# The first slice of a weight matrix loaded in two column halves, with two warm-up matmuls fewer

## The chip, the cores and the metric

The kernel runs on one core of a Trainium2 chip. The metric is the device time of one execution in microseconds (us).

## The reference

x has 4096 rows of 512 (128 batches of 32). For each row the reference computes

```python
base   = x @ W.T                                  # W 512 x 512
logits = x @ Wr.T + 5.0 * one_hot(language_of_batch)   # 8 experts
gates  = softmax over the two largest logits, 0 elsewhere
h      = x @ A[e].T for each expert e             # 8 experts x 16
c      = base + 2.0 * sum_e gates[e] * h[e] @ B[e].T
out    = x + softplus(scale) * (c @ sign)         # sign 512 x 512, of +1 and -1
```

all of it in fp32.

## The kernel before, in words

The kernel folds matrices first and then runs over the rows. It computes M = softplus(scale) * (W.T @ sign) + I once, and B2 = 2 * softplus(scale) * (B @ sign) once; then each of the 32 tiles of 128 rows needs x @ [Wr, A, M] (a product of width 648, held in two PSUM banks), the gates, and a small product h_gated @ B2 that is added to the same banks. Every fp32 operand is split in a rounded high part (suffix _hi, type fp32r) and the rest (suffix _lo), and a product is the sum of three: high by high, high by low and low by high.

The order of work is written out by hand, one list for each engine, tied together with semaphores. The part around the change is the opening, in which M is summed over four slices of 128 rows of W and sign (j = 0 to 3):

- **SyncE's queue** (lines 254 to 268) issues W's slices 0 and 1, the scale, W's slices 2 and 3, sign's slice 3, then the first tile of x, A, B and further tiles of x.
- **ScalarE's queue** (line 354) issues sign's slices 0, 1 and 2, then loads its activation table (line 357), and then makes w_hi of slice 0 in two operations (lines 362 and 364), w_hi of the other slices (line 367) and sign_hi of slices 1 to 3 (line 370).
- **VectorE** (lines 468 to 473) clears buffers, waits for sign's slice 0, and makes its sign_hi in two column halves of 256 (lines 493 and 494); each half has a semaphore of its own, first_sign_made and early_sign_hi_made. Behind it in the same list come w_lo of slice 0 and 1 (low_w, line 478), the scale (lines 499 to 501), w_lo of slice 2, eight operations on one column for softplus, w_lo of slice 3, the transposes of x, A, Wr and the language numbers (lines 488 and 521 to 526), then fold(k) (line 532), which reads the four finished sums of M, and low_m (line 538), which makes wide_lo, the low part of M.
- **GpSimd** builds the diagonals and makes sign_lo of each slice (line 318), for slice 0 when early_sign_hi_made says that the second half of sign_hi is there, for the others behind ScalarE's sign_hi.
- **TensorE** first runs WARM_UPS = 19 matmuls of constants (line 657), 128 x 256 bf16, whose result isn't used. Then come slice 0's high by high in column halves (lines 692 and 696): the four matmuls of the left half wait for the first half of w_hi and for first_sign_made, the four of the right half for early_sign_hi_made. Behind them stand low_high(0) (line 677, waits for w_lo of slice 0), high_high(1) (670), high_low(0) (684, waits for sign_lo of slice 0) and so on in a fixed order, slice 3 last (lines 650 to 652), then B2 (717, 721), then the first tile of x (first_tile, line 759) and the loop over tiles (wide, line 734, and lora, line 770). lora of tile 0 waits for ht_lo (line 569).

```python
            for j in range(EARLY):                      # EARLY = 1, VectorE
                dve.wait_ge(sign_loaded[j], 16)
                nc.vector.tensor_copy(sign_hi[:, j, 0:HALF], ...).then_inc(first_sign_made, 1)
                nc.vector.tensor_copy(sign_hi[:, j, HALF:D], ...).then_inc(early_sign_hi_made, 1)
                low_w(j)
            low_w(1)
```

Of the kernel before, what the change touches and what calls it, by code (L numbers as in the profile page):

```python
# [18 lines left out]
def adaln_ffn_kernel(nc: bass.Bass, x, lang_ids, W, Wr, A, B, sign, scale, out):  # L19
# [13 lines left out]
    BATCH, TILES, D = x.shape  # L33
# [5 lines left out]
    OC = O // P  # L39
# [2 lines left out]
    Y0 = D // 2  # L42
    BANKS = ((0, 0, HEAD + Y0), (1, HEAD + Y0, WIDE))
    assert BATCH == P and ER == P and D % (NQ * Q) == 0 and HEAD + Y0 <= 512 and O == KC * P
    WARM_UPS = 19
    HALF = D // 2
    EARLY = 1
    RING = 4
# [4 lines left out]
    sign_load = sign.rearrange("(j p) n -> p j n", p=P)  # L53
# [5 lines left out]
    with ctx:  # L59
        def sb(name, shape, dt=FP32):  # L60
            return ctx.enter_context(nc.sbuf_tensor(name, shape, dt))

        def sem(name):
            return ctx.enter_context(nc.semaphore(name))
# [3 lines left out]
        sign_in = sb("sign_in", [P, OC, D])  # L68
# [13 lines left out]
        sign_hi = sb("sign_hi", [P, OC, D], FP32R)  # L82
# [48 lines left out]
        a_loaded = sem("a_loaded")  # L131
        wr_loaded = sem("wr_loaded")
        w_loaded = [sem(f"w_loaded{j}") for j in range(OC)]
        sign_loaded = [sem(f"sign_loaded{j}") for j in range(OC)]
        b_loaded = sem("b_loaded")
        scale_loaded = sem("scale_loaded")
# [20 lines left out]
        first_sign_made = sem("first_sign_made")  # L157
# [193 lines left out]
        @block.scalar  # L351
        def _(act):

            for j in range(OC - 1):
                act.dma_start(sign_in[:, j, :], sign_load[:, j, :]).then_inc(sign_loaded[j], 16)

            nc.scalar.preload_act_table_set("natural_log_exp_and_others")
# [101 lines left out]
        def _(dve):  # L459
# [15 lines left out]
            def low_w(j):  # L475

                dve.wait_ge(w_hi_made, j + 1)
                nc.vector.tensor_tensor(w_lo[:, j, :, :, :],  # L478
                                        w_in[:, j, :].rearrange("p (i k a) -> p k i a", i=NQ, k=KC),
                                        w_hi[:, j, :, :, :].bitcast(FP32), ALU.subtract).then_inc(w_lo_made, 1)  # L480
# [8 lines left out]
                                    x_in[n][:, :, :].rearrange("p g c -> p (g c)")).then_inc(xt_made, 1)  # L489

            for j in range(EARLY):
                dve.wait_ge(sign_loaded[j], 16)
                nc.vector.tensor_copy(sign_hi[:, j, 0:HALF], sign_in[:, j, 0:HALF]).then_inc(first_sign_made, 1)
                nc.vector.tensor_copy(sign_hi[:, j, HALF:D], sign_in[:, j, HALF:D]).then_inc(early_sign_hi_made, 1)
                low_w(j)
            low_w(1)
# [150 lines left out]
        def _(pe):  # L647
# [7 lines left out]

            for _ in range(WARM_UPS):
                nc.tensor.matmul(p_b2[:, 0:2 * P], nc.const_aps.tensor(1.0, [P, P], BF16),
# [205 lines left out]
```

## Time and profile before

| | us |
|---|---|
| median of 3 runs | 163.86 (163.75 to 163.94) |
| the profiled execution, its own time | 163.53 |
| its span, first to last instruction | 161.3 |
| TensorE busy in it | 157.4 (98%) |
| VectorE busy | 110.0 (68%) |
| ScalarE busy | 63.6 (39%) |
| GpSimd busy | 52.2 (32%) |

Times in the rows are microseconds from the span's start unless marked ns. PE is TensorE's matmul side, PEld its weight loads, DVE VectorE, ACT ScalarE, POOL GpSimd, SP SyncE; a q behind a name is that engine's instruction queue, and L12 is line 12 of the kernel. Durations of matmuls include the way through the array, so those of neighbours overlap, and the distance of their starts is the pace. The page's row of TensorE's granted clock stands at 9 (90% or more) in all 40 slices.

### The profile page before, as it was taken

Reading aid. Unit: us, or ns where it says so; the run is one execution under the profiler, and the core shown is the slowest. Engines: PE = TensorE matmul, PEld = TensorE weight load, DVE = VectorE, ACT = ScalarE, POOL = GpSimd, SP = SyncE. Lnnn points to the kernel's source line nnn. Section 1 sums busy time; section 2 is a strip of 40 time slices with the busy share of each in tenths; the row PEclk is TensorE's granted clock in tenths of the full one; section 3 lists DMA queues with packets and bytes.
Section 4 is the critical chain, followed back from the end, with each engine's and each line's share of the span. In section 5 each row is a group of like instructions: output and inputs, shape, how many; then the busy total and the mean of one; then the engine's idle time right before and its main releaser. Section 6 shows DMA issues by size and latency. Waiting matters only on the chain.

```text
span 161.3 us, 3653 instructions
## 1 busy us (share of the span) xinstructions
PE 157.4 (98%) x1046; PEld 151.8 (94%) x1046; DVE 110.0 (68%) x451; ACT 63.6 (39%) x178; POOL 52.2 (32%) x50
## 2 busy tenths in 40 slices
PE   8999999999999999999999999999999999999993
PEld 5887889899999999999999999999999999999992
DVE  5999999566666667666656666676666666666641
ACT  3645622244433334234344444433444343334432
POOL 2975554333330323333333333223132333333000
PEclk9999999999999999999999999999999999999999
DMA  5995332335545545344454545555555362223333
GB/s 178 376 150 131 107 107 74 89 76 150 147 142 148 142 104 180 106 135 123 126 142 136 139 142 146 143 146 145 144 146 145 86 189 81 62 62 87 130 130 130
DMA packets 45867, 21.47 MB, mean 133 GB/s; under 512 B 23680, under 2 KB 40864, under 8 KB 45856
## 3 DMA queue, kind: packets, MB, share of 16 engines
q1 hardware_dynamic: 30232, 13.58, 31.0%
q10 hardware_dynamic: 15624, 7.76, 16.6%
q8 instruction: 5, 0.08, 0.2%
q14 instruction: 6, 0.05, 0.1%
HBM read 11.03 MB, written 8.39 MB: 120 GB/s over the span
## 4 chain that ended last, share of the span: by engine, by line
PE 78%; DVE 11%; DMA 4%; issue 1%; SPq 1%; ACT 1%; ACTq 0%; DVEq 0%
PE pair L734 63%; PE pair L770 15%; DMA w_in<-in_L_cond_W 2%; DVE wide_lo L538 2%; DMA h_moved<-h_gated 2%; DVE m_full L532 2%; DVE w_lo L478 1%; DVE xt L488 1%; SPq L277 1%; DVE scale_spread L499 1%; DVE b_lo L543 1%; DVE second L616 1%; ACT w_hi L367 0%; ACT xt_hi L383 0%; DVE wide_lo L548 0%
## 5 line engine op out<-in xcount | busy, mean ns | idle before, releaser
L325 POOL TENSOR_TENSOR xt_lo<-xt,xt_hi 128x512 fp32r<-128x512 f32 x32 | 41.8, 1305 | 90.2 <-ACT xt_hi L383 90.2
L734 PE MATMUL pair<-wide_hi,xt_lo 128*128 128x392 f32 (+1 forms) x248 | 58.5, 311 | 0.0
L734 PE MATMUL pair<-wide_hi,xt_hi 128*128 128x392 f32 (+1 forms) x248 | 58.4, 311 | 0.0
L734 PE MATMUL pair<-wide_lo,xt_hi 128*128 128x392 f32 (+1 forms) x248 | 58.4, 312 | 0.0
L734 PEld LDWEIGHTS pair<-wide_hi,xt_hi 128*128 128x128 f32 x248 | 38.6, 188 | 0.4 <-issue 0.3
L734 PEld LDWEIGHTS pair<-wide_hi,xt_lo 128*128 128x128 f32 x248 | 38.6, 188 | 0.0
L734 PEld LDWEIGHTS pair<-wide_lo,xt_hi 128*128 128x128 f32 x248 | 38.5, 188 | 0.0
L447 ACT ACTIVATE y<-pair 128x256 f32<-128x256 f32 x31 | 11.9, 383 | 50.1 <-PE pair L770 50.1
L383 ACT ACTIVATE xt_hi<-xt 128x512 fp32r<-128x512 f32 x32 | 20.3, 633 | 9.7 <-DVE xt L488 7.9
L488 DVE STREAM_TRANSPOSE xt<-x_in 128x512 f32<-128x512 f32 x32 | 22.5, 703 | 0.0
L421 ACT ACTIVATE ht_hi<-ht 128x128 fp32r<-128x128 f32 x29 | 12.6, 433 | 24.1 <-DVE ht L580 24.1
L569 DVE TENSOR_TENSOR ht_lo<-ht,ht_hi 128x128 fp32r<-128x128 f32 x29 | 13.1, 451 | 13.0 <-ACT ht_hi L421 13.0
L591 DVE TENSOR_TENSOR logits<-pair,bias 128x8 f32<-128x8 f32 x32 | 5.3, 166 | 24.0 <-PE pair L734 24.0
L770 PE MATMUL pair<-b_hi,ht_hi 128*128 128x256 f32 x64 | 13.7, 293 | 0.2 <-DVE ht_lo L569 0.2
L627 DVE SCALAR_TENSOR_TENSOR h_gated<-pair,rdenom,gate 128x128 f32<-128x128 f32 x32 | 11.2, 351 | 3.3
L770 PE MATMUL pair<-b_hi,ht_lo 128*128 128x256 f32 x64 | 13.0, 283 | 0.0
L770 PE MATMUL pair<-b_lo,ht_hi 128*128 128x256 f32 x64 | 12.9, 280 | 0.0
L449 ACT ACTIVATE y<-pair 128x256 f32<-128x256 f32 x32 | 12.2, 380 | 0.8 <-PE pair L770 0.8
L770 PEld LDWEIGHTS pair<-b_hi,ht_hi 128*128 128x128 f32 x64 | 9.9, 187 | 1.3 <-DVE ht_lo L569 0.7
L580 DVE STREAM_TRANSPOSE ht<-h_moved 128x128 f32<-128x128 f32 x29 | 9.0, 312 | 2.0 <-DMA h_moved<-h_gated 0.6
L616 DVE TENSOR_SCALAR second<-expert_no,top_no,e 128x8 f32<-128x8 f32 x32 | 10.1, 316 | 0.0
L770 PEld LDWEIGHTS pair<-b_lo,ht_hi 128*128 128x128 f32 x64 | 10.0, 188 | 0.0
(97 smaller groups left out, 142.5 us busy)
## 6 DMA issues: line engine op xcount, KB each, us to landing
out<-y SPq DMA_DIRECT2D x31, 256.0 KB, 2.3
x_in<-in_x ACTq DMA_DIRECT2D x104, 64.0 KB, 2.2
h_moved<-h_gated SPq DMA_DIRECT2D x116, 16.0 KB, 1.8
x_in<-in_x SPq DMA_DIRECT2D x24, 64.0 KB, 2.1
w_in<-in_L_cond_W SPq DMA_DIRECT2D x4, 256.0 KB, 4.4
sign_in<-in_L_ffn_sign ACTq DMA_DIRECT2D x3, 256.0 KB, 4.3
sign_in<-in_L_ffn_sign SPq DMA_DIRECT2D x1, 256.0 KB, 5.6
a_in<-in_L_cond_A SPq DMA_DIRECT2D x4, 64.0 KB, 4.0
```

What stands on the lines that cost most here:

```text
L325: nc.gpsimd.tensor_tensor(xt_lo[n][:, :, :].rearrange("p j (g b) -> p g j b", g=NQ), xt[n][:, :, :, :], xt_hi[n][:, :, :].bitcast(FP32).re ...
L383: nc.scalar.activation(xt_hi[n][:, :, :].rearrange("p j (g b) -> p g j b", g=NQ), xt[n][:, :, :, :], ACT.Copy).then_inc(xt_hi_made, 1)
L421: nc.scalar.activation(ht_hi[:, :].rearrange("p (b g) -> p g b", g=NQ), ht[:, :, :], ACT.Copy)\
L447: nc.scalar.activation(y[n][:, 0:Y0], pair[n][0][:, HEAD:HEAD + Y0], ACT.Copy)\
L449: nc.scalar.activation(y[n][:, Y0:D], pair[n][1][:, 0:D - Y0], ACT.Copy).then_inc(y_copied, 1)
L488: nc.vector.transpose(xt[n][:, :, :, :].rearrange("p g j b -> p (g j b)"), x_in[n][:, :, :].rearrange("p g c -> p (g c)")).then_inc(xt_mad ...
L569: nc.vector.tensor_tensor(ht_lo[:, :].rearrange("p (b g) -> p g b", g=NQ), ht[:, :, :], ht_hi[:, :].bitcast(FP32).rearrange("p (b g) -> p ...
L580: nc.vector.transpose(ht[:, :, :].rearrange("p g b -> p (g b)"), h_moved[n][:, :, :].rearrange("p g c -> p (g c)")).then_inc(ht_made, 1)
L616: nc.vector.tensor_scalar(second[:, :], expert_no[:, :], top_no[:, 1:2], e2[:, 0:1], ALU.is_equal, ALU.mult).then_inc(second_made, 1)
L627: nc.vector.scalar_tensor_tensor(h_gated[n][:, :].rearrange("p (e r) -> p e r", e=E), pair[n][0][:, E:HEAD].rearrange("p (e r) -> p e r", ...
L734: last = nc.tensor.matmul(pair[n][bank][:, at0:at0 + hi - lo], l[:, k, :], w[:, k, lo:hi], start=(opens and k == 0 and l is xt_hi[n] and w ...
L770: last = nc.tensor.matmul(o, l[:, :], w[:, (0, Y0)[bank]:(Y0, D)[bank]], start=False, stop=stop, skip_group_check=True)
```

## The change

The first slice of sign is loaded by two transfers on ScalarE's queue, columns 0 to 255 and columns 256 to 511, the first with a semaphore of its own. VectorE waits for the first transfer ahead of its first cast and for the second transfer ahead of its second cast. There are 17 warm-up matmuls in place of 19.

```diff
-    WARM_UPS = 19
+    WARM_UPS = 17
@@ semaphores
+        first_sign_loaded = sem("first_sign_loaded")
@@ ScalarE
-            for j in range(OC - 1):
+            act.dma_start(sign_in[:, 0, 0:HALF], sign_load[:, 0, 0:HALF]).then_inc(first_sign_loaded, 16)
+            act.dma_start(sign_in[:, 0, HALF:D], sign_load[:, 0, HALF:D]).then_inc(sign_loaded[0], 16)
+            for j in range(1, OC - 1):
                 act.dma_start(sign_in[:, j, :], sign_load[:, j, :]).then_inc(sign_loaded[j], 16)
@@ VectorE
             for j in range(EARLY):
+                dve.wait_ge(first_sign_loaded, 16)
+                nc.vector.tensor_copy(sign_hi[:, j, 0:HALF], sign_in[:, j, 0:HALF]).then_inc(first_sign_made, 1)
                 dve.wait_ge(sign_loaded[j], 16)
-                nc.vector.tensor_copy(sign_hi[:, j, 0:HALF], sign_in[:, j, 0:HALF]).then_inc(first_sign_made, 1)
                 nc.vector.tensor_copy(sign_hi[:, j, HALF:D], sign_in[:, j, HALF:D]).then_inc(early_sign_hi_made, 1)
                 low_w(j)
```

## Rows read from the trace of the kernel before

**Rows 1.** The page's chain that ended last, by line.
```profile
PE pair L734 63%; PE pair L770 15%; DMA w_in<-in_L_cond_W 2%; DVE wide_lo L538 2%; DMA h_moved<-h_gated 2%; DVE m_full L532 2%; DVE w_lo L478 1%; DVE xt L488 1%; SPq L277 1%; DVE scale_spread L499 1%; DVE b_lo L543 1%; DVE second L616 1%; ACT w_hi L367 0%; ACT xt_hi L383 0%; DVE wide_lo L548 0%
```

**Rows 2.** TensorE's timeline at its two waits: start, length, what, count, [idle before, releaser].
```profile
22.28 0.57 PE L759 MATMUL pair<-wide_lo,xt_hi 128*128 128x392 f32 x2 [0.29 <-DVE wide_lo L538]
...
31.93 0.50 PE L770 MATMUL pair<-b_hi,ht_hi 128*128 128x256 f32 x2 [0.16 <-DVE ht_lo L569]
```

**Rows 3.** TensorE: warm-ups' durations in ns, then timeline: start, length, what, count.
```profile
L657 PE MATMUL pair<-const-bfloat16-1.0 x19: 314/417/417, 0.8 to 4.6; 128*128 128x256 bf16 x19
...
0.77 4.11 PE L657 MATMUL pair<-const-bfloat16-1.0 128*128 128x256 bf16 x19 [0.77 <-PEq L850]
4.66 0.71 PE L692 MATMUL pair<-sign_hi,w_hi 128*128 128x256 f32 x4
...
5.67 1.09 PE L677 MATMUL pair<-sign_hi,w_lo 128*128 128x512 f32 x4
...
12.98 0.47 PE L650 MATMUL pair<-sign_hi,w_hi 128*128 128x512 f32 x1
...
13.51 0.40 PE L652 MATMUL pair<-sign_hi,w_lo 128*128 128x512 f32 x1
```

**Rows 4.** Timeline of the other engines, 0 to 10.5 us, same columns.
```profile
0.74 1.37 ACTq L355 DMA_DIRECT2D sign_in<-in_L_ffn_sign  x3
...
2.14 1.28 ACT L357 ACT_TABLE_LOAD   x1 [2.14 <-issue]
...
3.95 0.42 ACT L362 ACTIVATE w_hi<-w_in 128x256 fp32r<-128x256 f32 x1 [0.53 <-DMA w_in<-in_L_cond_W]
4.13 0.38 DVE L493 CAST sign_hi<-sign_in 128x256 fp32r<-128x256 f32 x1 [0.76 <-DMA sign_in<-in_L_ffn_sign]
...
4.43 0.38 DVE L494 CAST sign_hi<-sign_in 128x256 fp32r<-128x256 f32 x1
...
4.73 0.77 DVE L478 TENSOR_TENSOR w_lo<-w_in,w_hi 128x512 fp32r<-128x512 f32 x1
4.94 3.42 POOL L318 TENSOR_TENSOR sign_lo<-sign_in,sign_hi 128x512 fp32r<-128x512 f32 x2
...
5.13 0.64 ACT L367 ACTIVATE w_hi<-w_in 128x512 fp32r<-128x512 f32 x1 [0.46 <-DMA w_in<-in_L_cond_W]
...
5.80 1.40 DVE L478 TENSOR_TENSOR w_lo<-w_in,w_hi 128x512 fp32r<-128x512 f32 x1 [0.30 <-ACT w_hi L367]
...
7.13 1.27 DVE L499 TENSOR_SCALAR scale_spread<-scale_spread,scale_rows 128x32 f32<-128x32 f32 x1
...
7.34 0.64 ACT L367 ACTIVATE w_hi<-w_in 128x512 fp32r<-128x512 f32 x1 [1.05 <-DMA w_in<-in_L_cond_W]
...
7.88 0.62 ACT L370 ACTIVATE sign_hi<-sign_in 128x512 fp32r<-128x512 f32 x1
...
8.57 1.30 POOL L318 TENSOR_TENSOR sign_lo<-sign_in,sign_hi 128x512 fp32r<-128x512 f32 x1 [0.21 <-ACT sign_hi L370]
...
8.81 1.61 DVE L478 TENSOR_TENSOR w_lo<-w_in,w_hi 128x512 fp32r<-128x512 f32 x1
```

**Rows 5.** DMA view of 1.7:3.5, 3.5:4.6, 4.6:5.5 and 7.6:8.6 us; last, 3.6:3.9 by queue.
```profile
DMA packets 259, 0.50 MB, mean 279 GB/s; under 512 B 14, under 2 KB 14, under 8 KB 259
...
DMA packets 247, 0.44 MB, mean 404 GB/s; under 512 B 30, under 2 KB 30, under 8 KB 247
...
DMA packets 188, 0.34 MB, mean 380 GB/s; under 512 B 21, under 2 KB 21, under 8 KB 188
...
DMA packets 584, 0.29 MB, mean 292 GB/s; under 512 B 65, under 2 KB 567, under 8 KB 584
...
q1 hardware_dynamic: 55, 0.11, 96.2%
q10 hardware_dynamic: 9, 0.00, 4.8%
```

**Rows 6.** VectorE's fold of the first finished sum, timeline from 14 us.
```profile
14.14 0.71 DVE L532 SCALAR_TENSOR_TENSOR m_full<-pair,sp,eye 128x512 f32<-128x512 f32 x1
```

## The prediction

> **What bounds the kernel now.** I read four views, in this order. The page's chain of waits comes first [rows 1]: 63% and 15% of the span are TensorE's matmuls of the tile loop, so from about 32 us on the time is TensorE's work and a shift that survives until then reaches the end in full. The list of who waited for whom is next; besides its start it has two waits of TensorE in the whole run, and the timeline puts them at 22.28 us (0.29 us for wide_lo, line 538) and at 31.93 us (0.16 us for ht_lo, line 569) [rows 2], both times for VectorE. These two are what is to be seen: up to 22 us the pace is set by VectorE's list of work, and TensorE, if it came to those places up to 0.29 + 0.16 = 0.45 us later, would lose nothing. The timeline of the opening [rows 3, 4] shows how both engines get there, and the DMA view by stretches [rows 5] how the first loads share the queues.
>
> TensorE's real work begins at 4.66 us, right behind 19 warm-ups [rows 3]. Of the two things it waits for, the first half of w_hi is ready at 3.95 + 0.42 = 4.37 us and the first half of sign_hi at 4.13 + 0.38 = 4.51 us, because sign's 256 KB land at 4.13 us and w's at 3.95 us [rows 4]. So VectorE's cast is the later one, and the change is aimed at that.
>
> **The start of TensorE.** Two warm-ups go. Their 19 take 4.11 us from the start of the first to the end of the last, which is 0.31 us long itself (the others 0.42) [rows 3]: eighteen steps of (4.11 - 0.31)/18 = 0.211 us. Without two of them the row ends about 0.42 us sooner, near 4.4 us. The first 128 KB of sign should be complete by 3.7 to 3.9 us (below), its cast by 4.1 to 4.3. One more issue stands on ScalarE's queue: three take 1.37 us, 0.46 each [rows 4], so the table load moves from 2.14 to 2.60 us and ends at 3.88 us. It was covered by the wait for w until 3.95 us and still is, by 0.07 us; without that cover it would cost its excess. Then w_hi's first half, at 4.37 us or a little sooner, is the last to come, and TensorE starts at about 4.48 us, 0.15 to 0.18 us sooner.
>
> **The second half of sign.** It is a transfer of its own behind the first, and what matters is when it lands, Lb. Before, all of it was there at 4.13 us. Bounds: if it follows the first half with nothing in between, only the smaller packets cost. In 4.6 to 5.5 us, 167 of the 188 packets were of 2 KB, on 16 engines in 0.9 us, 86 ns each; in 7.6 to 8.6 us 519 of 584 held 512 bytes or more, 31 ns each [rows 5]; a packet of 1 KB lies between, an estimate of 50 ns. Sixteen of those for eight of 86 ns per engine are 0.11 us more: Lb = 4.2. At the other end, w's second slice, issued ahead of it, gets all its turns first, 8 x 86 = 0.69 us more, and the queue of ScalarE pauses as it did from 3.6 to 3.9 us, when it moved 9 packets (its end-of-transfer ones) against 55 of the other queue [rows 5]: Lb = 5.1. Between them I go by bytes. Up to 3.5 us 0.50 MB had moved, up to 4.6 us another 0.44 MB [rows 5], and w's second slice, whose last packets fall there, was used at 5.13 us [rows 4], half a microsecond later. The four transfers w0, sign's two halves and w1 are 0.75 MB; the last 0.25 MB at 404 GB/s end at 4.1 us, plus 0.1 for small packets, plus 0.53 to landing: Lb = 4.75. The pause speaks for this middle: w's second slice makes use of it, so the second half won't overtake it, nor wait for all of it.
>
> The Trainium skill, DMA: Bandwidth & Descriptors, section Queues, rings and completion order, has each engine alternate between rings only after a whole packet of some 9 to 17 descriptors. By that rule all of w1's share comes ahead of the second half, and the second half would land near 4.9 us; that both queues are served in one stretch is seen here, how finely they alternate on one engine is not.
>
> **What is queued behind that wait.** VectorE stands at the new wait with its own list behind it: cast of the second half, w_lo of slice 0, w_lo of slice 1, scale, w_lo of slice 2. Call X the time the second cast ends: 4.43 + 0.38 = 4.81 before, Lb + 0.40 after, so 5.15. Two strings of work hang on X.
>
> VectorE and GpSimd: their large operations never run together. w_lo of slice 1 starts at 5.80 us and takes 1.40 us where w_lo of slice 0 takes 0.77, since sign_lo holds it; scale_spread, 128x32, takes 1.27 us, until sign_lo's second one ends at 8.36; w_lo of slice 2 starts at 8.81, 0.24 us behind sign_lo's third (8.57), and takes 1.61 us [rows 4]. So the order is one serial string: w_lo 0, sign_lo 0, w_lo 1, sign_lo 1, scale. It starts at X - 0.08 and scale ends at X + 3.59. But the next link is tied elsewhere: sign_lo's third waits for sign_hi of slice 2 (7.88 + 0.62 = 8.50), which waits for w's third slice, landed by 7.34 us; its bytes are behind the same number of bytes as before, so I leave it, plus 0 to 0.1 us. VectorE is through w_lo 2 at 8.57 + 1.85 = 10.42 us as long as the string reaches sign_lo's third by 8.57, which is X up to 5.07. Beyond, it goes as X + 5.35. With X = 5.15: 10.50, so +0.08 us.
>
> TensorE: its second halves of slice 0 can't start ahead of X + 0.11 (sign_lo's first, the other that waits for this cast, begins at 4.94, 0.13 us behind it), and low_high of slice 0 (5.67 us) waits for w_lo 0, which ends at X + 0.69. So it is late by X - 4.81 + 0.03 = 0.37 us there: the 0.17 us won at the start are lost in a gap between the halves. It has slack later. At 12.98 us it waits for w_lo of slice 3: two steps take 0.53 us where 2 x 0.23 would do (three steps of line 677 take 1.09 - 0.39 = 0.70), with an idle 0.03 about 0.1 us. And the first sum is complete at 13.51 + 0.40 = 13.91 us while VectorE takes it up at 14.14 us [rows 3, 6], 0.23 us. Together 0.33 us: of 0.37 us, 0.04 reach VectorE. Afterwards both run as before, and the 0.45 us of [rows 2] cover TensorE's own lateness again.
>
> **Sum.** The larger of 0.08 and 0.04 us, with some of the 0 to 0.1 us of w's third slice: +0.1 us. The profiled execution is 163.53 us (span 161.3), so 163.63 by its own time; the median of the runs shown, 163.86, lies 0.33 above it, and I forecast 163.96 us. A measurement of this kernel can tell about 0.2%, 0.33 us, from no change.
>
> **Rivals.** (a) The second half lands late, Lb 5.0 to 5.1 or more, because the third transfer on the queue isn't let in until an earlier one has landed, as sign's second slice started only at 3.9 us. The mechanism is the in-order wait on VectorE that holds w_lo 0 and with it sign_lo 0; it decides from X = 5.07, and its price is X - 5.07. At Lb = 5.1, X = 5.5: +0.43, 164.3 us. For it: the pause in [rows 5]. Against it: bytes flow at 404 GB/s around that pause, so w1's packets get done in it and are out of the way. Chance of more than 0.33 us this way: 0.2.
> (b) The order on the shared port flips in the kernel's favour. If the second half lands by 4.17 us, X is 0.24 us earlier and w_lo 2 starts ahead of sign_lo's third instead of behind it: 0.85 us less on VectorE, of which the first sum (13.91 - 0.17) lets 0.23 + 0.17 = 0.40 through, and the 0.45 us of waits give that back: 163.46 us. Against it: the low bound of Lb has to hold. A like flip comes if w's third slice is later relative to the string. Chance 0.17. The Trainium skill, SBUF — State Buffer, has these two engines take one port pair in turns, the loser blocked entirely; by that rule the flip is all or nothing, and this trace agrees (1.27 us for 128x32).
> (c) Nothing is to be seen: the second half comes between 4.2 and 4.67 us, TensorE starts sooner and meets the same two waits: 163.86 us. Chance 0.22.
> (d) The clock. The warm-ups' 0.211 us for 256 columns is the lower level, 1.2 GHz, the four matmuls behind them step by (0.71 - 0.28)/3 = 0.14 us, the upper one, 2.4 GHz [rows 3]; the rise falls at the last warm-up, with TensorE busy without a hole. Now it meets a hole between the halves of up to 0.5 us. If the rise came as much later as it took from the start, 3.8 us, half of that is lost, 1.9, less the slack of 0.33: 165.4 us. Against it: the rise before fell ahead of where the hole will be. Chance 0.05.
> That the change doesn't split the wait at all can't be: the second cast, not the first, stands behind sign_loaded.
>
> **How the numbers follow.** The forecast (Lb 4.67 to 5.0, 0 to +0.33 us) has 0.36, (c) 0.22, (a) 0.2, (b) 0.17, (d) 0.05. Of (b), all counts as faster, 0.17; (a) and (d) with a little for w's third slice coming later, 0.27, as slower; the rest, 0.56, is within 0.2%. The range goes from (b)'s 163.46 to 0.45 us above the median, 164.4, and leaves out (d) and the tail of (a).
>
> **What would show it.** Right: the warm-ups end near 4.4 us, the first real matmul at 4.5; a gap in TensorE before line 696's second halves; the cast of the second half at 4.8 us instead of 4.4; sign_lo's first at 5.3; w_lo 2 still ending at 10.4 to 10.5 us; the wait for wide_lo again at 22.3. Wrong: a second cast by 4.5 us, w_lo 2 in less than 1 us, or matmuls at the warm-ups' pace behind 4.6 us.

## The result, and the profile after

The changed kernel takes 164.57 us (median of 20 runs, 163.91 to 165.88) against 163.94 us for the kernel before (20 runs): ratio 1.0038, 95% interval 1.0023 to 1.0053, 0.63 us more. The forecast was 163.96 us with a range to 164.4. The profiled execution took 164.41 us against 163.53, so 0.88 us more, with a span of 162.2 us.

First the page's chain and the waits of TensorE in the changed kernel (columns: us in total, times, longest), the counterparts of [rows 1] and of the waits in [rows 2]. Its line numbers stand 3 or 4 above those of before: ScalarE's 373 for 370, TensorE's 674, 681, 688, 696 and 763 for 670, 677, 684, 692 and 759.

```profile
PE pair L738 63%; PE pair L774 15%; DMA sign_in<-in_L_ffn_sign 3%; DMA h_moved<-h_gated 2%; DVE wide_lo L542 2%; PE pair L688 2%; DVE m_full L536 2%; PE pair L674 1%; SPq L278 1%; PE pair L681 1%; DVE xt L491 1%; DVE second L620 1%; ACT sign_hi L373 0%; ACT xt_hi L386 0%; DVE wide_lo L552 0%
```
```profile
PE pair L674 <- ACT sign_hi L373: 1.0, 1, 1.0
PE pair L661 <- PEq L854: 0.8, 1, 0.8
PE pair L774 <- DVE ht_lo L573: 0.2, 1, 0.2
```

The wait for wide_lo is gone. A wait of 1.0 us for sign_hi of **slice 1** is there in its place, and the chain's first load is one of sign where it was one of W. The timeline of the opening shows the place:

```profile
1.18 0.45 ACTq L356 DMA_DIRECT2D sign_in<-in_L_ffn_sign  x1
...
1.65 0.94 ACTq L358 DMA_DIRECT2D sign_in<-in_L_ffn_sign  x2
...
2.62 1.28 ACT L360 ACT_TABLE_LOAD   x1 [2.62 <-issue]
...
3.89 0.36 DVE L496 CAST sign_hi<-sign_in 128x256 fp32r<-128x256 f32 x1 [0.51 <-DMA sign_in<-in_L_ffn_sign]
3.92 0.42 ACT L365 ACTIVATE w_hi<-w_in 128x256 fp32r<-128x256 f32 x1
...
4.39 0.80 PE L696 MATMUL pair<-sign_hi,w_hi 128*128 128x256 f32 x4
...
4.91 0.29 DVE L498 CAST sign_hi<-sign_in 128x256 fp32r<-128x256 f32 x1 [0.66 <-DMA sign_in<-in_L_ffn_sign]
5.12 2.39 DVE L481 TENSOR_TENSOR w_lo<-w_in,w_hi 128x512 fp32r<-128x512 f32 x2
...
5.86 1.20 PE L681 MATMUL pair<-sign_hi,w_lo 128*128 128x512 f32 x4
...
7.31 0.63 ACT L373 ACTIVATE sign_hi<-sign_in 128x512 fp32r<-128x512 f32 x1 [1.94 <-DMA sign_in<-in_L_ffn_sign]
...
8.08 1.16 PE L674 MATMUL pair<-sign_hi,w_hi 128*128 128x512 f32 x4 [1.03 <-ACT sign_hi L373]
...
8.66 1.19 DVE L481 TENSOR_TENSOR w_lo<-w_in,w_hi 128x512 fp32r<-128x512 f32 x1 [0.51 <-ACT w_hi L370]
...
9.71 2.67 POOL L319 TENSOR_TENSOR sign_lo<-sign_in,sign_hi 128x512 fp32r<-128x512 f32 x2 [0.40 <-ACT sign_hi L373]
```

Up to 5.86 us all of it is close to the forecast: the table load from 2.62 us, TensorE's first real matmul at 4.39 (4.48 forecast), the second cast over at 4.91 + 0.29 = 5.20 (X = 5.15 forecast), low_high of slice 0 0.19 us later than before (0.37 forecast). Then ScalarE stands 1.94 us in front of slice 1 of sign, which lands at 7.3 us; before, sign_hi of slice 1 ran at 5.67 us and found it there. TensorE has nothing to do from 7.1 to 8.1 us, its high_high of slice 1 starts at 8.08 us where it started at 6.60, and the first sum of M, taken up by VectorE at 14.14 us before [rows 6], is late by 1.35 us (timeline of the changed kernel):

```profile
15.49 0.75 DVE L536 SCALAR_TENSOR_TENSOR m_full<-pair,sp,eye 128x512 f32<-128x512 f32 x1 [1.07 <-PE pair L656]
```

Of these 1.35 us 0.9 reach the end of this execution. On VectorE the rest is gone by its second fold, which starts at 17.46 us for 16.58, 0.88 us late, because b_lo between the two folds took 0.68 us in place of 1.16. On TensorE it goes at the wait for wide_lo of [rows 2]: the matmuls of tile 0 that read wide_lo start 1.41 us late, those of tile 1 behind them 0.88 us. The wait for ht_lo stays, at 0.20 us. The lines are one of VectorE and two of TensorE from the kernel before, then the same three from the changed kernel (timelines):

```profile
14.77 1.16 DVE L543 TENSOR_TENSOR b_lo<-b_in,b_hi 128x512 fp32r<-128x512 f32 x1
20.94 1.05 PE L759 MATMUL pair<-wide_lo,xt_hi 128*128 128x392 f32 x6
22.68 0.47 PE L734 MATMUL pair<-wide_hi,xt_hi 128*128 128x392 f32 x2
...
16.16 0.68 DVE L547 TENSOR_TENSOR b_lo<-b_in,b_hi 128x512 fp32r<-128x512 f32 x1
22.35 1.38 PE L763 MATMUL pair<-wide_lo,xt_hi 128*128 128x392 f32 x8
23.56 0.46 PE L738 MATMUL pair<-wide_hi,xt_hi 128*128 128x392 f32 x2
```

The DMA view of 4.6 to 5.5 us, the counterpart of the third row of [rows 5], shows engines that are not full:

```profile
DMA packets 124, 0.21 MB, mean 232 GB/s; under 512 B 22, under 2 KB 22, under 8 KB 124
```

It was 188 packets and 380 GB/s. The trace records the landing of such a transfer as 16 events, one for each share of it. Of slice 1's 16 shares 14 land between 5.1 and 5.7 us and the last two at 6.95 and 7.29 us; two 2 KB packets on ScalarE's queue that began at 4.3 to 4.4 us took 836 and 1084 ns, where 84 is usual.

### The profile page after: what moved, and what is told of

It is laid out like the page before. It is cut to its first block, busy times and chain, and to the rows that moved or that the text cites. A ratio compares the mean times of both kernels' runs of the same rounds, so it can differ in the third digit from the quotient of the medians.

```text
span 162.2 us, 3650 instructions
## 1 busy us (share of the span) xinstructions
PE 157.4 (97%) x1044; PEld 151.7 (93%) x1044; DVE 109.0 (67%) x451; ACT 63.9 (39%) x178; POOL 50.9 (31%) x50
## 4 chain that ended last, share of the span: by engine, by line
PE 83%; DVE 7%; DMA 5%; ACT 1%; SPq 1%; ACTq 1%; issue 1%; DVEq 0%
PE pair L738 63%; PE pair L774 15%; DMA sign_in<-in_L_ffn_sign 3%; DMA h_moved<-h_gated 2%; DVE wide_lo L542 2%; PE pair L688 2%; DVE m_full L536 2%; PE pair L674 1%; SPq L278 1%; PE pair L681 1%; DVE xt L491 1%; DVE second L620 1%; ACT sign_hi L373 0%; ACT xt_hi L386 0%; DVE wide_lo L552 0%
```

## The experiments

All ratios are to the kernel before on the same chip, with the 95% interval in brackets. "Slice 1" is sign's; its time is the start of ScalarE's sign_hi of it where that waited for the load.

**1. The two halves of the change.**

```diff
# split19: the change with     WARM_UPS = 19
# whole17: the kernel before with
-    WARM_UPS = 19
+    WARM_UPS = 17
```

> The change with its 19 warm-ups kept. Queue theory (the extra transfer makes sign's slice 1 land late, 7.29 us in the changed kernel's profile against 5.46 before, and TensorE waits 1.0 us for it): still slower by the whole of the change, ratio 1.003 to 1.005. Warm-up theory (two fewer let TensorE idle and the clock suffers): back to 1.000. Late-cast theory (only the second cast's end, X, matters): as the change or 0.0 to 0.1 us worse, since 19 warm-ups end at 4.9 us.

> 17 warm-ups, sign's slice 0 in one transfer. Queue theory and late-cast theory: 1.000, TensorE starts at 4.6 us as before, with a hole of 0.1 us behind the warm-ups. Warm-up theory: 1.003 or more, with matmuls at the lower level's pace behind 4.6 us.

split19: 1.0027 [1.0005, 1.0050], +0.98 us by the medians; whole17: 0.9995 [0.9975, 1.0016]. So two warm-ups fewer cost nothing that can be seen, and what costs is the split. That the first real matmul stood at 4.40 us in split19's profile, with 19 warm-ups, doesn't show that 19 fit: in that execution the clock rose at 3.4 us and shortened the last of them. In the profile of both (below), where it rose late, 19 of them lasted until 4.98 us.

**2. The split, without a cast that runs ahead, and an extra transfer elsewhere.**

```diff
# both: 19 warm-ups, two transfers for slice 0, one wait for both
-                dve.wait_ge(sign_loaded[j], 16)
+                dve.wait_ge(sign_loaded[j], 32)
# latesplit: the kernel before, slice 1 in two column halves, ScalarE waits for 32
+            act.dma_start(sign_in[:, 1, 0:HALF], sign_load[:, 1, 0:HALF]).then_inc(sign_loaded[1], 16)
+            act.dma_start(sign_in[:, 1, HALF:D], sign_load[:, 1, HALF:D]).then_inc(sign_loaded[1], 16)
```

> Slice 0 in two transfers, VectorE waits for both ahead of the first cast, 19 warm-ups. Queue theory: slower by 0.3 to 0.6 us, slice 1 late again. Late-cast theory: the whole opening waits for the second half (4.9 us against 4.1), so X = 5.6 and +0.5 us, with slice 1 used at its old time, 5.7 to 6.0 us.

> Slice 0 in one transfer as before, slice 1 in two, both waited for together: one transfer more on the queue, but not ahead of the first cast. Queue theory: slices 1 and 2 land later than before (by 0.2 to 1.5 us) and the kernel is slower by 0.2 to 0.6 us. Late-cast theory: 1.000, X stays 4.8 us.

both: 1.0055 [1.0031, 1.0080]. In its profile slice 1 was not badly late (5.83 us), but TensorE's first real matmul stood at 5.38 us, X was 5.43 and W's third slice was used at 7.90 us (7.34 before), so this kernel doesn't part the theories. latesplit: 1.0003 [0.9983, 1.0023], its own time 163.31 us. An extra transfer behind slice 0, even of 1 KB packets, costs nothing that can be seen. Against the queue theory as I had put it, slice 2 in that profile landed late (7.0 us) and was in nobody's way.

**3. Rows in place of columns.**

```diff
+            act.dma_start(sign_in[0:64, 0, :], sign_load[0:64, 0, :]).then_inc(sign_loaded[0], 16)
+            act.dma_start(sign_in[64:P, 0, :], sign_load[64:P, 0, :]).then_inc(sign_loaded[0], 16)
```

> Slice 0 in two transfers of 64 rows (2 KB packets, as before) in place of two column halves, both waited for ahead of the first cast, 19 warm-ups. In the three kernels with column halves of slice 0 the 16 DMA engines are not full between 5.0 and 5.8 us and the last of slice 2's 16 shares lands at 7.7 to 9.0 us for 6.2. Small-packet theory (1 KB packets beside 2 KB ones upset the order of the queues): no hole at 5.0 to 5.8 us, 1.000, since the bytes ahead of each transfer are the same. Extra-transfer theory: the hole stays, +0.3 to 0.9 us.

1.0086 [1.0054, 1.0119], the reverse of what small packets would make of it. It isn't a clean test, since the issues themselves got longer (ScalarE's four to 3.17 us in place of 2.62, timeline of rowsplit), so that w_hi began only behind the table load at 4.46 us, and the first cast at 5.65 us:

```profile
0.74 0.56 ACTq L354 DMA_DIRECT2D sign_in<-in_L_ffn_sign  x1
1.32 0.61 ACTq L355 DMA_DIRECT2D sign_in<-in_L_ffn_sign  x1
1.98 1.16 ACTq L357 DMA_DIRECT2D sign_in<-in_L_ffn_sign  x2
3.17 1.28 ACT L359 ACT_TABLE_LOAD   x1 [3.17 <-issue]
4.46 0.42 ACT L364 ACTIVATE w_hi<-w_in 128x256 fp32r<-128x256 f32 x1
```

**4. The late cast alone.** A clearing of a spare 128x512 buffer between VectorE's two casts, in the kernel before.

```diff
+                nc.vector.memset(pad[:, :], 0.0)
                 nc.vector.tensor_copy(sign_hi[:, j, HALF:D], sign_in[:, j, HALF:D]).then_inc(early_sign_hi_made, 1)
```

> The kernel before with one clearing of 128x512 put between VectorE's two casts: the transfers stay as they are, X (the end of the second cast) goes from 4.8 to 5.2 us, as in the changed kernel. Late-cast theory: as slow as the change, 1.0038. By the string of the prediction: 0.1 us. Queue theory: 1.000 to 1.001, so that nearly all of the change's 0.63 us is the late slice 1.

0.9989 [0.9972, 1.0005]. Timeline of pause:

```profile
5.23 0.22 DVE L496 CAST sign_hi<-sign_in 128x256 fp32r<-128x256 f32 x1
5.38 2.38 DVE L479 TENSOR_TENSOR w_lo<-w_in,w_hi 128x512 fp32r<-128x512 f32 x2
...
6.36 1.09 PE L679 MATMUL pair<-sign_hi,w_lo 128*128 128x512 f32 x4
...
9.36 1.35 DVE L479 TENSOR_TENSOR w_lo<-w_in,w_hi 128x512 fp32r<-128x512 f32 x1
```

The second cast ends at 5.45 us, 0.64 us later than before and 0.25 us later than in the changed kernel; low_high of slice 0 moves from 5.67 to 6.36 us, and the time doesn't. The upper end of the interval, 1.0005, lies below the change's 1.0038. So the wait that the change adds on VectorE is not what it costs.

**5. The late slice 1 alone.** Three copies of it into a spare buffer on ScalarE, ahead of its sign_hi, in the kernel before.

```diff
                     act.wait_ge(sign_loaded[j], 16)
+                    if j == 1:
+                        for i in range(3):
+                            nc.scalar.activation(pad[:, i, :], sign_in[:, j, :], ACT.Copy)
```

> The kernel before with three copies of 128x512 into a spare buffer put on ScalarE ahead of sign_hi of slice 1, which then ends at 8.0 us in place of 6.3, as in the changed kernel (7.94). The transfers are as before. If the late sign_hi of slice 1 is what the change costs: slower by 0.5 to 0.8 us, 1.003 to 1.005, with TensorE waiting 1.0 to 1.2 us at high_high of slice 1. If the cost lies elsewhere: 1.000.

1.0059 [1.0034, 1.0084], +1.06 us by the medians; TensorE waits 1.5 us in the profile, half a microsecond more than in the changed kernel:

```profile
7.54 0.61 ACT L374 ACTIVATE sign_hi<-sign_in 128x512 fp32r<-128x512 f32 x1
...
8.30 1.16 PE L674 MATMUL pair<-sign_hi,w_hi 128*128 128x512 f32 x4 [1.52 <-ACT sign_hi L374]
```

With no transfer touched, holding back sign_hi of slice 1 (and with it ScalarE's list behind it) makes the whole cost and more.

**6. Why it is late.** Three kernels on the changed one: the second half issued by SyncE behind W's slice 1 (spsecond); SyncE's issue of the scale moved behind W's slice 2 (scale2); sign's slice 1 issued by SyncE behind W's slice 1 (sp1).

```diff
# spsecond, SyncE, behind W's slice 1 (and taken from ScalarE)
+                    sp_eng.dma_start(sign_in[:, 0, HALF:D], sign_load[:, 0, HALF:D]).then_inc(sign_loaded[0], 16)
# scale2
-                if j == 1:
+                if j == 2:
                     sp_eng.wait_ge(rows_zeroed, 2)
# sp1, SyncE, behind W's slice 1 (and taken from ScalarE)
+                    sp_eng.dma_start(sign_in[:, 1, :], sign_load[:, 1, :]).then_inc(sign_loaded[1], 16)
```

> The change with the second half issued by SyncE behind w's slice 1, so that ScalarE's queue goes from the first half to slice 1 at once. Queue theory: slice 1 starts at 3.4 us and lands before 5.0, TensorE doesn't wait for sign_hi of slice 1; but the second half lands near 5.0 to 5.3 us, X = 5.5, so 0.3 to 0.5 us slower than before by the late cast. If slice 1 lands late here too, its place on the queue isn't what matters.

> The change with SyncE's issue of the scale moved behind w's slice 2, which is then issued at 1.65 us in place of 2.41. In the changed kernel SyncE's queue has nothing to move from 4.2 to 4.9 us and ScalarE's slice 1 runs alone. If the late slice 1 comes from that empty queue: w's slice 2 starts at 4.2 us, the 16 engines stay full, slice 1 lands by 5.8 us, and the kernel is within 0.1% of before. If not: the same hole and 1.003 to 1.005.

> The change with sign's slice 1 issued by SyncE behind w's slice 1 in place of ScalarE behind the second half. If the place behind the two halves on ScalarE's queue makes slice 1 late: it lands by 5.6 us, no wait of TensorE at 8 us, 1.000 to 1.002 of before. If the reads of slice 1 are slow wherever they are issued: last share above 6.5 us and 1.003 to 1.006.

spsecond: 1.0153 [1.0122, 1.0184]. Slice 1 was in time (sign_hi at 5.74 us, behind w_hi without a wait), but now the second half came at 6.28 us, later than I had expected of it. TensorE stood still for 1.47 us, and what followed ran at the lower clock (stretches of spsecond; the clock is the figure behind POOL's):

```profile
5.00:6.00 1.00, 0.17 (x2) 0.00 (x0) 0.00 (x0) 0.80 (x2) 0.00 (x0) 1.00 1.07 393
6.00:7.00 1.00, 0.37 (x3) 0.37 (x4) 0.72 (x2) 0.35 (x1) 0.34 (x1) 1.00 1.02 389
7.00:8.00 1.00, 1.00 (x6) 0.90 (x5) 1.00 (x2) 0.86 (x2) 1.00 (x1) 0.51 1.05 377
8.00:9.00 1.00, 1.00 (x4) 0.81 (x3) 1.00 (x2) 0.29 (x1) 1.00 (x2) 0.50 1.25 198
```

That is rival (d) of the prediction, made by a longer hole than the change itself has (the changed kernel's clock is 0.998 over the span). It is only a part of spsecond's cost: four of its six runs had a granted clock of 0.987 to 0.990 over the span and took 166.6 to 167.1 us, the other two 0.998 and 1.0 and took 165.9 and 166.0. scale2: 1.0054 [1.0034, 1.0075]. The DMA engines were busier this time (376 GB/s in 4 to 5 us, where the changed kernel had 321), and slice 1 was late all the same, 7.23 us: the empty queue isn't needed for it. Part of that may be sharing, since W's slice 2 now runs beside slice 1, whose thirteenth share landed at 6.16 us against 5.54. sp1: 1.0041 [1.0016, 1.0066], slice 1 at 6.81 us: nor is ScalarE's queue needed. (In sp1's profile TensorE had no wait for slice 1. The clock rose only at 6.7 us there, which made TensorE itself late.)

What the three share is the **order of issue over both queues**. Before, without the scale, which is a few bytes, it is W0, sign 0, then W1 and sign 1 within 0.01 us of each other, then sign 2; with the halves, sign 1 is the fifth transfer issued. (In scale2, W's slice 2 and sign 1 are issued within 0.01 us, as fifth and sixth; their last shares landed at 7.04 and 7.21 us.) In spsecond the second half is the fifth, and it is the late one. Three further kernels put that to the test:

```diff
# allhalf: the change with slice 1 in two column halves too
# swap12: the change with slice 2 issued ahead of slice 1
-            for j in range(1, OC - 1):
+            for j in (2, 1):
# w1half: the kernel before with W's slice 1 in two column halves
+                    sp_eng.dma_start(w_in[:, 1, 0:HALF], w_load[:, 1, 0:HALF]).then_inc(w_loaded[1], 16)
+                    sp_eng.dma_start(w_in[:, 1, HALF:D], w_load[:, 1, HALF:D]).then_inc(w_loaded[1], 16)
```

> The change with slice 1 in two column halves too. In latesplit slice 1 in halves landed by 5.1 us. If what stalls is the start of 2 KB packets behind 1 KB ones: slice 1 by 5.6 us and 1.000 to 1.002, the stall moves to slice 2. If it is the place behind slice 0's halves: last share of slice 1 above 6.5 us, 1.003 to 1.006.

> The change with slice 2 issued ahead of slice 1 on ScalarE's queue. If the transfer directly behind the halves is the one that stalls: slice 2 has a share that lands more than 1 us behind its thirteenth. If it belongs to slice 1: slice 1 has it, wherever it stands. Either way slice 1 is late by its new place (6.2 us or more), and the kernel slower than the change, 1.004 to 1.010.

> The kernel before with W's slice 1 in two column halves on SyncE's queue, both waited for together. If halves that run beside full transfers upset the loads whatever the matrix: some share of a later transfer lands 1 us or more late and 1.002 to 1.006. If only slice 0 of sign does: 1.000.

(The 5.1 us of latesplit in the first of them was that of 16 of its 32 shares; the last landed at 5.84 us.) allhalf: 1.0035 [1.0011, 1.0059], slice 1 at 6.88 us, so no matter of 2 KB behind 1 KB packets; a fifth issue also moved its table load to 3.16 us and made TensorE wait 0.7 us for w_hi. swap12: 1.0098 [1.0063, 1.0132], slice 1 at 7.61 us, and slice 2 in the fifth place had its last share at 6.57 us, 0.7 us behind its thirteenth, less than I had put as the mark. w1half: 1.0031 [1.0005, 1.0058]: here W's slice 1 is late, whose second half is the fifth transfer (timeline of w1half, against 5.13 us in [rows 4]):

```profile
6.38 0.63 ACT L371 ACTIVATE w_hi<-w_in 128x512 fp32r<-128x512 f32 x1 [1.60 <-DMA w_in<-in_L_cond_W]
```

In the traces of the five kernels that leave all slices whole (before, whole17, pause, actpause and, below, order_b) the last share of the fourth transfer, sign 1, landed at 5.5 to 5.8 us, and that of the fifth, sign 2, at 6.2, 7.0, 6.5, 6.5 and 7.4 us, where it has time until 7.9 us. So a straggling fifth isn't new with the change. The change puts a transfer there that is wanted at 5.7 us. One profile speaks against the place as the whole reason: in latesplit the fifth transfer issued is the second half of slice 1, and the last share of slice 1 landed at 5.84 us, in time for sign_hi at 5.96, at a ratio of 1.0003. So a transfer in the fifth place is often late, not always, and what decides it isn't shown.

**7. The wait filled.** TensorE's high_low of slice 0 ahead of high_high of slice 1, on the changed kernel (order_a) and on the one before (order_b).

```diff
             low_high(0)
-            high_high(1)
             high_low(0)
+            high_high(1)
```

> The change with TensorE's high_low of slice 0 ahead of high_high of slice 1. It needs sign_lo of slice 0 (6.96 us in the changed kernel) and fills the 1.0 us in which TensorE waits for slice 1. If that wait is the cost: back to 1.000 to 1.001 of before, the wait at 8.1 us gone or below 0.2 us. If VectorE's and ScalarE's lists are late by themselves: no change against the changed kernel, 1.004.

> The same swap in the kernel before, the control. TensorE would wait about 0.1 us more for sign_lo of slice 0 (6.69 against 6.6 us), which the later waits cover: 1.000, at best 0.1% less.

order_a: 1.0028 [1.0005, 1.0052]; order_b: 1.0015 [0.9991, 1.0039]. The wait was gone, but the intervals don't part order_a from the change or from the kernel before. So the changed kernel was measured again, and a third time beside order_a:

> The changed kernel once more, for a second profile. If the late slice 1 belongs to the change: its last share lands above 6.5 us again, TensorE waits 0.8 us or more at 8 us, ratio 1.002 to 1.006. If it was an accident of one execution: last share by 5.9 us and no wait.

> The changed kernel a third time. Place theory (with the halves, slice 1 is the fifth transfer issued in place of the fourth, and single shares of the fifth land 1 us or more late): its last share above 6.5 us, TensorE waits 0.5 us or more at high_high of slice 1, 1.002 to 1.005. If the change costs nothing on most chips: 1.000 to 1.001.

> The change with the two groups of matmuls swapped, beside again2 on the same chip. Place theory: slice 1 is as late, the wait is filled, and it is 0.1 to 0.3% faster than again2. If the wait isn't the cost: equal to again2.

again: 1.0006 [0.9983, 1.0030]; again2: 1.0042 [1.0023, 1.0060]; order_a2: 1.0029 [1.0011, 1.0047], its median 164.11 us against 164.38 for again2 and 163.70 for the kernel before. Two of three measurements of the change agree. The second saw nothing by the ratio, though slice 1 was late in its profile (7.27 us). The profiles say more than the ratios. That of again2 is one in which the fifth transfer was in time (timeline):

```profile
5.70 0.63 ACT L373 ACTIVATE sign_hi<-sign_in 128x512 fp32r<-128x512 f32 x1 [0.34 <-DMA sign_in<-in_L_ffn_sign]
...
14.29 0.71 DVE L536 SCALAR_TENSOR_TENSOR m_full<-pair,sp,eye 128x512 f32<-128x512 f32 x1
```

and that of order_a2 one in which it was late and TensorE had other work (timeline):

```profile
6.98 1.19 PE L688 MATMUL pair<-sign_lo,w_hi 128*128 128x512 f32 x4
...
7.26 0.63 ACT L373 ACTIVATE sign_hi<-sign_in 128x512 fp32r<-128x512 f32 x1 [1.95 <-DMA sign_in<-in_L_ffn_sign]
...
8.04 1.15 PE L674 MATMUL pair<-sign_hi,w_hi 128*128 128x512 f32 x4
...
14.55 0.71 DVE L536 SCALAR_TENSOR_TENSOR m_full<-pair,sp,eye 128x512 f32<-128x512 f32 x1
```

Side by side, each profiled execution by its own time:

| kernel | first four real matmuls take | sign_hi of slice 1 starts | first fold | lora of tile 0 starts | us |
|---|---|---|---|---|---|
| before | 0.71 | 5.67 | 14.14 | 31.93 | 163.53 |
| whole17 | 0.74 | 5.96 | 14.17 | 32.03 | 163.94 |
| the change, again2 | 0.81 | 5.70 | 14.29 | 32.01 | 163.53 |
| the change | 0.80 | 7.31 | 15.49 | 32.84 | 164.41 |
| the change, again | 1.21 | 7.27 | 15.45 | 32.91 | 164.72 |
| split19 | 0.80 | 7.27 | 15.44 | 32.79 | 164.84 |
| actpause | 0.71 | 7.54 | 15.70 | 33.27 | 164.98 |
| order_a | 0.92 | 7.41 | 14.67 | 32.19 | 163.82 |
| order_a2 | 1.04 | 7.26 | 14.55 | 32.07 | 163.66 |

In these executions the same program costs nothing where slice 1 is in time and 0.9 to 1.2 us where it isn't, and with the wait filled a slice 1 as late as that costs 0.1 to 0.3 us. A single execution's time can differ by some 0.4 us for reasons behind the opening (whole17 starts lora 0.10 us late and takes 0.41 us more), so the column of lora, behind which the views show no wait of TensorE in these executions, is the safer one: 0.08 us late where slice 1 is in time, 0.86 to 0.98 where it isn't, 0.14 and 0.26 with the wait filled. The column of the first matmuls tells when the clock rose in that execution (last section); it doesn't go with the time. The medians recover less than the profiles. Against the kernel before, order_a and order_a2 still take 0.1 and 0.3% more (ratios 1.0028 and 1.0029), and what costs that was not found; neither interval parts the swapped kernel from the change.

## Why the prediction was wrong

- **The start of TensorE**: right. 4.39 us against 4.48 forecast, 4.66 before; the table load ended at 3.90 us and stayed covered.
- **The second half of sign**: right. It was cast at 4.91 us, Lb = 4.9 (4.75 forecast, 4.2 to 5.1 as bounds; the upper one leaves out the 0.11 us for small packets that the lower one has), in time for X = 5.20 (5.15). The Trainium skill's rule on the turns of the rings (DMA: Bandwidth & Descriptors, Queues, rings and completion order) gave an estimate of 4.9, which is what was measured here. In the other profiles with this order of issue the last share of the second half landed at 4.74 to 4.92 us, so they can't tell the rule from an estimate 0.15 us away.
- **The string on VectorE and GpSimd**: its form was right in pause, its price too high. For X = 5.45 it gave +0.38 us; w_lo of slice 2 ended 0.29 us late there (10.71 us), lora of tile 0 started 0.16 us late, and the ratio was 0.9989. (By the prediction's own rows the string meets sign_lo's third at X = 5.02, since sign_lo's second ends at 8.36 = X + 3.55, not at 5.07.) In the changed kernel the string didn't bind at all: with slice 1 late, w_lo of slice 2 came ahead of sign_lo's third and ended at 9.85 us (10.4 to 10.5 forecast). That is the flip of rival (b), and it brought nothing, because VectorE then waited 1.07 us for TensorE at the first fold. Rival (a), which was to be the way to a slower kernel, is refuted as a cause: the outcome was on its side, by another mechanism.
- **The step that failed** is in the part on what the second half's transfer moves. I went through W's third slice, "its bytes are behind the same number of bytes as before, so I leave it", and did not go through sign's slice 1 at all, the transfer directly behind the added one, although TensorE's high_high of slice 1 needs it next. By bytes it would have been as early as before; in the changed kernel its last share landed at 7.29 us for 5.46, TensorE waited 1.03 us for it, and high_high of slice 1 began 1.48 us late. It moved from the fourth to the fifth issue, and of the nine profiles in which it follows two column halves of slice 0 on ScalarE's queue, sign_hi of it starts at 6.9 to 7.4 us in seven and at 5.7 and 5.8 in two. Its slack was small: sign_hi of slice 1 ended at 6.29 us before and TensorE took it up at 6.60. W's third slice, for which the sum has 0 to 0.1 us, was off too: it landed at 7.97 us for 7.32, and 0.5 us late in again2, where nothing came of it.
- **The 0.33 us of slack and the 0.45 us of later waits**: right in kind, too large in part. Of the slack ahead of the first fold 0.13 us showed (1.48 us late at slice 1, 1.35 at the fold). Of the two waits only the one for wide_lo was used up; the one for ht_lo moved along and stayed 0.20 us. The way from 1.35 to 0.88 us on VectorE, a shorter b_lo, is not in the prediction.
- **The clock**: rightly small for the change. That the rise falls at the last warm-up was read from one execution and holds for that one alone; it moves about (last section). spsecond shows that a fall behind a longer hole can happen, and what it costs, about 1 us.
- **The warm-ups**: costless, as forecast.

The range ended at 164.4 because the tail of rival (a) was the only slow case in it. (That is 0.45 us above the forecast; above the median of the runs shown, as the prediction says, it would be 164.3.) The case that came true, a later transfer pushed back by the added one, was not among the rivals.

Open: why single shares of the fifth transfer lag by 1 us or more. The step from small to large packets, the empty SyncE queue and ScalarE's queue are not needed for it by allhalf, scale2 and sp1, each by one profile; whether it is the memory, the engines or the supply of descriptors no run here shows. That the place in the order decides rests on the pattern over the profiles, with latesplit against it, not on a kernel that changes it alone. What is shown is one step nearer: a late slice 1 makes the cost (actpause, and the table above).

## What to carry to other kernels

When a load is cut in two, price each load that is issued behind it by who waits for it and with what slack, not only the two halves; the added issue can make the next transfer late even when no byte is added (here in seven of nine profiles). Where loads straggle by chance, order the consumer so that it has other work to do at that point (here one swap of matmul groups turned a wait of 1 us into none in the profiles; the ratios don't show the gain apart from noise). And take more than one profile where the first one shows a load far off its usual time.

## What the runs showed of the hardware

- One DMA's 16 shares don't land together: in the first microseconds of loads the last one came up to 1.8 us behind the thirteenth (slice 1 in order_a, 5.59 and 7.39 us; in the changed kernel 5.54 and 7.29), with single 2 KB reads of 0.8 to 1.3 us beside the usual 84 ns.
- A transfer over 64 partitions took longer to issue than one over 128 with the same number of shares, 16: 0.56 and 0.61 us in rowsplit against 0.40 and 0.45 us before.
- The clock's rise to 2.4 GHz, with TensorE busy since 0.77 us each time, came at 3.4 us in one execution (split19), at 6.2 us in another (again), where the first four real matmuls took 1.21 us in place of 0.80, and at 6.7 us in sp1. In again the wait for slice 1 took that up: it was 0.71 us in place of 1.03, and the first fold came at 15.45 us, not later than in the changed kernel.
- In spsecond TensorE, idle for 1.47 us until 6.63 us, had a granted clock of about 0.50 from 7 to 10 us; in the changed kernel a hole of 1.03 us did not bring it down.
